# Rotary products of an attention stage move from VectorE to ScalarE and GpSimd, and two steps of the pipeline change place

## The reference, cut to what matters

```python
qkv = x @ w_qkv.T + b_qkv ;  Q, K, V = split(qkv)
Q, K = rope(Q), rope(K)          # x1*cos - x2*sin, x1*sin + x2*cos
iq = x @ w_iq.T + b_iq           # 4 heads of 64
ik = x @ w_ik.T + b_ik ;  iw = x @ w_iw.T + b_iw
index_scores = sum_h relu(iq_h . ik) * iw_h
mask = top 32 of index_scores per row
attn = softmax(Q K^T / sqrt(128) + (0 where mask else -inf))
x = x + (attn @ V) @ w_o.T + b_o
```

## Time and profile before

| | us |
|---|---|
| median of 3 runs (1388.53 to 1389.38) | 1388.75 |
| the profiled execution | 1393.16 |
| its span, first to last instruction | 1391.3 |

### The profile page before, as it was taken

The page is one execution under the profiler, slowest core; times in us unless marked ns, Lnnn a source line. Parts: engine busy times, 40 slices in busy tenths (PEclk is TensorE's granted clock), DMA queues, the critical chain, the costliest instruction groups (busy, mean ns, idle before and its releaser), DMA issues. The chain is left out here.

```text
span 1391.3 us, 20802 instructions
## 1 busy us (share of the span) xinstructions
PE 1074.8 (77%) x4202; PEld 628.9 (45%) x4203; DVE 957.2 (69%) x2340; ACT 723.1 (52%) x1759; POOL 778.0 (56%) x586
## 2 busy tenths in 40 slices
PE   4877776335999995588889898988775509999996
PEld 3656664324777772232333333333222505555563
DVE  4979899741333332589999999999998624555574
ACT  2554454432555544786676757677431205555542
POOL 0111110077713727895978888787964367627476
PEclk9998998556999997699998999999999558999998
DMA  8993000014633432444443453534441016635335
GB/s 242 158 176 93 1 1 0 1 48 58 89 63 66 88 68 36 104 123 141 132 149 120 142 165 119 159 121 153 160 143 45 19 46 86 91 71 95 84 69 103
DMA packets 136879, 133.22 MB, mean 96 GB/s; under 512 B 14579, under 2 KB 117603, under 8 KB 136675
## 3 DMA queue, kind: packets, MB, share of 16 engines
q1 hardware_dynamic: 107106, 115.55, 31.2%
q0 software_dynamic: 29696, 16.86, 9.5%
HBM read 98.66 MB, written 31.60 MB: 94 GB/s over the span
## 5 line engine op out<-in xcount | busy, mean ns | idle before, releaser
L1573 POOL TENSOR_TENSOR ss_HC<-ss_Hs,ss_Cb 128x512 f32<-128x512 f32 x256 | 317.6, 1270 | 94.2 <-PE ss_Y L1347 72.3
L1347 PE MATMUL ss_Y<-ss_HC,g_ident 128*128 128x512 f32 x512 | 268.7, 640 | 48.0 <-POOL ss_HC L1573 39.9
L1642 DVE TENSOR_TENSOR_SCAN ss_Hs<-ss_dA,ss_dBu 128x512 f32<-128x512 f32 x256 | 297.1, 1202 | 6.6 <-ACT ss_dA L1489 6.6
L996 PE MATMUL m_x_UP<-g_m_w,m_x_gT 128*128 (+1 forms) x532 | 204.6, 491 | 6.0 <-issue 2.4
L1489 ACT ACTIVATE ss_dA<-ss_delta,g_A 128x510 f32<-128x510 f32 x256 | 167.7, 712 | 59.5 <-DVE ss_Hs L1642 59.3
L1347 PEld LDWEIGHTS ss_Y<-ss_HC,g_ident 128*128 128x128 f32 x512 | 89.5, 196 | 212.2 <-POOL ss_HC L1573 155.2
L1634 DVE TENSOR_TENSOR ss_dBu<-ss_duP,ss_Bb 128x512 f32<-128x512 f32 x256 | 163.5, 686 | 22.0 <-DMA ss_Bb<-bc_rows 17.8
L1016 PEld LDWEIGHTS m_x_DP<-g_m_w,m_x_hT 128*128 128x128 f32 (+1 forms) x908 | 131.3, 189 | 79.9 <-issue 37.0
L1016 PE MATMUL m_x_DP<-g_m_w,m_x_hT 128*128 (+3 forms) x908 | 161.1, 295 | 5.3 <-ACT m_x_hT L1072 2.7
L1099 DVE SCALAR_TENSOR_TENSOR m_x_hid<-m_x_UP,m_x_G,m_x_sg 128x352 f32<-128x352 f32 x78 | 45.5, 584 | 154.7 <-ACT m_x_sg L1054 154.7
L976 POOL DMA_INDIRECT g_X<-out_rows,g_slot x64 | 99.1, 1549 | 76.6 <-DMA out_rows<-m_x_YO 54.0
(11 more groups left out here) (241 smaller groups left out, 1871.2 us busy)
## 6 DMA issues: line engine op xcount, KB each, us to landing
ss_Bb<-bc_rows SPq DMA_DIRECT2D x64, 512.0 KB, 4.9
ss_Cb<-bc_rows SPq DMA_DIRECT2D x64, 512.0 KB, 4.1
rows<-g_Z SPq DMA_DIRECT2D x2, 5031.0 KB, 54.3
m_x_G<-rows SPq DMA_DIRECT2D x156, 64.5 KB
out_rows<-m_x_YO SPq DMA_DIRECT2D x156, 64.0 KB
g_m_w<-in_w_up SPq DMA_DIRECT2D x1, 2816.0 KB, 10.2
g_m_b<-in_b SPq DMA_DIRECT2D x1, 2160.0 KB, 12.2
g_X<-in_x SPq DMA_DIRECT2D x4, 512.0 KB, 5.9
```

The source lines that it names most:

```text
L996: ins = nc.tensor.matmul(UP[v % 2][:, at:at + n], gT[v % 2][:], w.w[:, ds(e + c, n)], start=True, stop=True)
L1347: ins = nc.tensor.matmul(Yp[:, h, :], ident[:], HC[n % 2][:, h, :], start=False, stop=n == N - 1)
L1573: nc.gpsimd.tensor_tensor(HC[n % 2][:, h, :], Hs[n % 4][:, h, :], Cb[g % 2][:, n % 2, :], ALU.mult).then_inc(hc_ready.sem, 1)
L1642: v_.tensor_tensor_scan(Hs[n % 4][:, h, :], dA[n % NA][:, h, :, :].rearrange("p s t -> p (s t)"), dBu[:, h, :], 0.0, ALU.mult, ALU.add).th ...
```

## The change

Three things change. ScalarE's exponentials of unit s-2 move from behind the rows of s+1 to the place right behind the copy of xT, ahead of everything else of the step. VectorE's four rotary instructions go; in their place ScalarE copies each of the four 128x256 blocks with its bias (Identity) into RP, and GpSimd multiplies the whole of RP (128x1024) in place by the cosines and sines, waits for that, and adds as before. VectorE's update of a unit comes one step later, between choose rounds 0 and 1. The loop now holds steps 3 to 14.

```diff
@@ -170,7 +170,7 @@
         iq_ready = m.sig("iq_ready")
         ikv_ready = m.sig("ikv_ready")
         rope_parts = m.sig("rope_parts", 4)
-        qk_sum = m.sig("qk_sum")
+        qk_sum, rotated = m.sig("qk_sum"), m.sig("rotated")
         iq_copied = m.sig("iq_copied", 2)
         ikv_copied = m.sig("ikv_copied", 2)
         vo_ready = m.sig("vo_ready")
@@ -199,10 +199,10 @@
 
             step(0, 0, True, False, False)
             step(1, 1, True, True, False)
+            step(2, 2, True, True, True)
             with eng.Fori(0, (B - 4) // 4) as i:
                 for k in range(4):
-                    step(4 * i + 2 + k, (2 + k) % 4, True, True, True)
-            step(B - 2, 2, True, True, True)
+                    step(4 * i + 3 + k, (3 + k) % 4, True, True, True)
             step(B - 1, 3, True, True, True)
             step(B, 0, False, True, True)
             step(B + 1, 1, False, False, True)
@@ -313,6 +313,19 @@
                     if front:
                         act.wait_ge(xT_ready.sem, xT_ready.after(s))
                         nc.scalar.activation(xT[v][:], b0[:, 0:W2], ACT.Copy).then_inc(xT_copied.sem, 1)
+                    if tail:
+                        act.wait_ge(negmax.sem, negmax.after(s - 2))
+                        for t in range(2):
+                            nc.scalar.activation(PR[v][:, t * S:(t + 1) * S], MK[v][:, t * S:(t + 1) * S], ACT.Exp,
+                                                 bias=mx[v][:, t:t + 1], scale=scale,
+                                                 accum_out=rsum[v][:, t:t + 1]).then_inc(probs_ready.sem, 1)
+                    if front:
+                        act.wait_ge(qk_ready.sem, qk_ready.after(s))
+                        if not (first and s < 2):
+                            act.wait_ge(qk_sum.sem, qk_sum.after(s - 2))
+                        for k in range(4):
+                            nc.scalar.activation(RP[v][:, k * S:(k + 1) * S], (b12a, b12b)[k // 2][:, k % 2 * S:(k % 2 + 1) * S],
+                                                 ACT.Identity, bias=bias[:, k:k + 1]).then_inc(rope_parts.sem, 1)
                         act.wait_ge(iq_ready.sem, iq_ready.after(s))
                         for k in range(2):
                             nc.scalar.activation(IQ[v][:, k * S:(k + 1) * S], b3[:, k * S:(k + 1) * S], ACT.Identity,
@@ -325,12 +338,6 @@
                         nc.scalar.activation(VO[q][:], b0[:, 0:W2], ACT.Copy).then_inc(vo_copied.sem, 1)
                         if not (first and s == B - 1):
                             normalise(s + 1, 1 - v)
-                    if tail:
-                        act.wait_ge(negmax.sem, negmax.after(s - 2))
-                        for t in range(2):
-                            nc.scalar.activation(PR[v][:, t * S:(t + 1) * S], MK[v][:, t * S:(t + 1) * S], ACT.Exp,
-                                                 bias=mx[v][:, t:t + 1], scale=scale,
-                                                 accum_out=rsum[v][:, t:t + 1]).then_inc(probs_ready.sem, 1)
                     for t in range(2):
                         if front:
                             act.wait_ge(scores_ready.sem, scores_ready.after(s, t + 1))
@@ -349,15 +356,6 @@
 
             @block.vector
             def _(dve):
-                def rotate(s, v):
-
-                    dve.wait_ge(qk_ready.sem, qk_ready.after(s))
-                    for k in range(4):
-                        nc.vector.scalar_tensor_tensor(RP[v][:, k * S:(k + 1) * S],
-                                                       (b12a, b12b)[k // 2][:, k % 2 * S:(k % 2 + 1) * S],
-                                                       bias[:, k:k + 1], rope[:, k // 2 * S:(k // 2 + 1) * S],
-                                                       ALU.add, ALU.mult).then_inc(rope_parts.sem, 1)
-
                 def head_weights(s, v):
 
                     dve.wait_ge(vo_copied.sem, vo_copied.after(s))
@@ -426,20 +424,17 @@
                     if middle:
                         index_scores(s - 1, u)
                         choose(s - 1, u, range(0, 1))
-                    if front:
-                        rotate(s, v)
+                    if tail and not (isinstance(s, int) and s < 3):
+                        update(s - 3, u)
                     if middle:
-                        choose(s - 1, u, range(1, 3))
-                    if middle:
-                        choose(s - 1, u, range(3, TOPK // 8))
+                        choose(s - 1, u, range(1, TOPK // 8))
                     if front:
                         head_weights(s, v)
                     if middle:
                         mask(s - 1, u)
-                    if tail:
-                        update(s - 2, v)
 
                 steps(dve, step)
+                update(B - 1, 1)
 
             @block.gpsimd
             def _(pool):
@@ -455,6 +450,10 @@
                         x = X[:, ds(s * W2, W2)].rearrange("p (t d) -> p t d", d=D)
                         nc.gpsimd.tensor_tensor(x, x, b_o[:].unsqueeze(1).to_broadcast([P, 2, D]), ALU.add).then_inc(b_added.sem, 1)
                         pool.wait_ge(rope_parts.sem, rope_parts.after(s))
+                        parts = RP[v][:].rearrange("p (r k s) -> p r k s", r=2, k=2)
+                        nc.gpsimd.tensor_tensor(parts, parts, rope[:].rearrange("p (r s) -> p r s", r=2).unsqueeze(2).to_broadcast([P, 2, 2, S]),
+                                                ALU.mult).then_inc(rotated.sem, 1)
+                        pool.wait_ge(rotated.sem, rotated.after(s))
                         if not (isinstance(s, int) and s < 2):
                             pool.wait_ge(logits_ready.sem, logits_ready.after(s - 2))
                         nc.gpsimd.tensor_tensor(QK[v][:], RP[v][:, 0:2 * S], RP[v][:, 2 * S:4 * S], ALU.add).then_inc(qk_sum.sem, 1)
```

## The result

| | before | after |
|---|---|---|
| median, us (4 runs each) | 1388.64 (1384.98 to 1389.38) | 1357.64 (1356.96 to 1360.02) |
| the profiled execution, its span | 1393.16, 1391.3 | 1357.22, 1355.3 |

The ratio is 0.9773, with a 95% interval of 0.975 to 0.9797: 31.0 us less, where 22.6 were forecast.

A forecast was written before the change was run, and what follows sets the result against it. VectorE was taken to bound the attention, at 12.70 us per step. 23.6 us from 15 shorter periods, less 1.0 for lateness, made 22.6, from a median of 1388.75 to 1366 us; range 1361 to 1373.

The forecast's parts named there:

- VectorE sets the pace: In the attention loop, VectorE's queue was said to set the step's period of 12.70 us.
- it loses the rotary products: In VectorE's queue, 1.57 us go from each of units 1 to 15: 23.6 us, period 11.13.
- The update costs and gives nothing: VectorE's update, some 0.8 us, takes the same room one step later and does not wait; nothing taken for it.
- The exponentials fit into ScalarE's idle time and pay for the copies: On ScalarE, 0.98 us of exponentials use 2.95 us of idle time; relu starts at 145.17 against 145.49 despite 1.6 of copies.
- second loop: The attention's loop through TensorE and ScalarE, 11.3 to 11.6 us, was to become 10.9, 0.2 behind VectorE's 11.13.
- The rival that the second loop takes over: The loop through TensorE and ScalarE keeps 11.6 us, so the gain is only 16.5 us, 1372; chance 0.10.
- Lateness: Table loads on ScalarE and half-clock TensorE products, at loop heads and entry, cost 0 to 3.5 us; 1 taken.
- Gaps and clock: VectorE's 7.06 and 2.83 us gaps at the loop's jumps back stay; -4.2 to +4.2 us, no change taken.
- Exclusion of VectorE and GpSimd: Rival: each GpSimd product holds up a two-input VectorE index-score instruction; 37.6 us lost against 23.6 won, 1403; chance 0.03.
- the trace does not agree: Scan-stage VectorE scans beside GpSimd products, 1185 to 1222 ns throughout, were taken to contradict the skill page's exclusion rule.
- its milder form: GpSimd products hold VectorE only in steps behind the two jump gaps, under 5 us lost, 1371; no separate chance.

The follow-up runs named there:

- j2: The changed kernel with the reciprocals of the row sums made by GpSimd instead of VectorE; 1354.02 us, ratio to before 0.9751.
- i1: The changed kernel with the update back at the step's end, the loop over steps 2 to 13 and 60 do-nothing instructions ahead; 1359.52 us, ratio to before 0.979.
- e7: The changed kernel with the exponentials alone put back behind the rows of the next unit; 1366.22 us, ratio to before 0.983.
- e4: The kernel before with only the rotary products moved to ScalarE's copies and GpSimd's product; 1379.7 us, ratio to before 0.9938.
- g1: The kernel before with 50 do-nothing instructions ahead of VectorE's attention steps; 1378.92 us, ratio to before 0.9926.
- g2: The changed kernel with 40 do-nothing instructions ahead of VectorE's attention steps; 1370.43 us, ratio to before 0.9867.
- e1: The changed kernel with four semaphore increments added to each step of VectorE's loop body; 1357.48 us, ratio to before 0.9777.
- e3: The kernel before with the loop over steps 3 to 14 instead of 2 to 13; 1391.26 us, ratio to before 1.0032.
- e8: The changed kernel with a second, useless 128x1024 GpSimd product into a spare buffer in each unit; 1361.77 us, ratio to before 0.9799.
- h1: The changed kernel with an extra MAX8 over 768 constants between negmax and the index scores in each middle VectorE step; 1379.35 us, ratio to before 0.9928.
- e2: The kernel before with one common wait ahead of both MATCH_REPLACE8 of a round instead of one each; 1402.83 us, ratio to before 1.0102.

## Why the forecast was right in its mechanism and too small

- *VectorE sets the pace* and *it loses the rotary products*: right. 15 x 1.57 = 23.6 was forecast, 23.7 us came from the periods. That the two agree so well is in part luck: the steady step is 11.19, not 11.13, which makes 22.7, and 1.0 us came from the steps at and behind the loop heads, which I hadn't counted. j2 shows that VectorE still bounds the step.
- *The update costs and gives nothing*: right (i1).
- *The exponentials fit into ScalarE's idle time and pay for the copies*: right. The copies take 1.44 us to IQ's start where I took 1.6. ScalarE's part of the second loop takes 10.5 us where I took 10.9, and TensorE stands 0.21 us for the head weights, where I had the loop 0.2 behind VectorE's. e7 prices the move at 8.6 us. The rival that the second loop takes over is what e4 and e7 are.
- *Lateness, taken as 1 us of 0 to 3.5*: nothing was lost by it. The table loads in the attention went from three, one in each round of the loop, to one, at 39.58 us, and the granted clock there is 0.98, against 0.92 in the stretch to 247 us before. What caused the loads to go was not tested.
- *Gaps and clock, "I take no change", with 2 x 2.83 as the low end*: **this step failed.** The term was sized -4.2 to +4.2, and it measured -9.0, or -9.7 with the issue time inside the body. I had read the two gaps as what a jump back costs, so that the shorter row was the floor. By these runs it is what fetching the body again costs. Whether it is fetched is decided by where the body lies in VectorE's program (g1, g2, e1, e3), and the change pushed it from 150 to 199 by writing one more step out ahead of the loop, less the instructions that it dropped there. That is by chance: the same change 40 instructions later would have given 18.2 us (g2). The forecast's 22.6 and these 9.0 make 31.6, against 31.0 between the medians; that is closer than the parts are known, since between the two profiles the attention alone gives 33.3.
- *Exclusion of VectorE and GpSimd*, which I took to be contradicted by rows 7: wrong, though it did not decide. The second input of the scans in rows 7, dBu, lies in PSUM (line 1187), so they read one operand from SBUF and are no case of the rule. So "the trace does not agree" was a misreading. e8, g2 and h1 show the exclusion. It doesn't occur in after since the product starts 0.19 us behind the last L376, as the forecast had worked out (0.2). The chance of 0.03 was too low for a margin of that size, and its milder form, behind the gaps alone, is what g2 measured at 5.9 us; without gaps there was nothing to set it off.

The places of the table agree with blocks of 128 instructions, of which three are kept: if a block's border lies between places 189 and 199, and one each 128 places on, then after, e1, g1 and i1 touch three blocks, and before, e2, e3, e4 and g2 four. The border is worked out from these bodies, and what the hardware holds of a body was not measured by itself. The Trainium skill, page "Advanced Engine Details and Errata", section "ISA Cache", gives the cache as 32 KB in two lines of 16 KB, 256 instructions each (on TensorE 128 KB), and says that this can be configured for each engine. That is a rule that I should have weighed, since by it a jump back may or may not fetch. By its figures, 64 bytes for one, our packets of 8192 bytes are an estimated 128 instructions, half its line. With two lines of 256, e3 (not kept) and g1 (kept) would put a border between 316 and 331, and then before, 150 to 522, would be kept too; it isn't, so here the measurement decides against lines of that size; how the cache was configured in these runs isn't known.

## What to carry to other kernels

An "issue" gap behind a loop's jump is not a fixed price: count the engine's instructions ahead of and inside the loop, and expect any edit that shifts or resizes it to win or lose the whole gap, so the bound of that term reaches to nothing. Before a row is taken as evidence against a rule, look at where each operand lives. And when work moves to an engine off the path, look for the idle time it goes into; the reordering that made room for it was worth 8.6 us here.

## What the runs showed of the hardware that was not expected

- 50 instructions that do nothing, ahead of a loop, made the kernel 10.0 us faster (g1); 40 of them made another 12.8 slower (g2).
- Where the body is fetched again, VectorE stands for 3.0 to 8.8 us at the first jump back and for 2.8 to 3.0 at the second; where it is kept, for 0.15 to 0.52 at either.
- A scalar_tensor_tensor of 0.48 us with two SBUF inputs takes up to 2.58 beside a GpSimd product of 2.35, and GpSimd's takes 2.83 when VectorE was first. One GpSimd instruction holds one of VectorE's: in h1 the next was held by the addition (1.50 us beside 1.27). The Trainium skill, page "SBUF — State Buffer", section "Who interferes with whom", says that the first to issue has the shared ports for its whole instruction; by that, the trace agrees.
- On GpSimd a power of 128x2 takes 0.70 us in j2, and a product of 128x1024 2.35.
